# Decay products with gate masks in three bf16 parts in place of one fp32 product

## The reference, cut to what matters

```python
g = -jnp.exp(A_log) * jax.nn.softplus(a + dt_bias)      # one gate per token and value head
def step(S, xs):
    qt, kt, vt, gt, bt = xs
    S = S * jnp.exp(gt)[..., None, None]
    kS = jnp.einsum('bhk,bhkv->bhv', kt, S)
    S = S + bt[..., None, None] * kt[..., :, None] * (vt - kS)[..., None, :]
    o = jnp.einsum('bhk,bhkv->bhv', qt, S)
    return (S, o)
```

## Time and profile before

| | |
|---|---|
| median of 3 runs | 2314.36 us (2313.28 to 2314.37) |
| the profiled execution | 2313.63 us, span 2311.6 us |
| busy: PE | 2015.2 us, 87% |
| busy: DVE | 1538.9 us, 67% |
| busy: ACT | 982.5 us, 43% |
| busy: POOL | 758.4 us, 33% |
| mean granted TensorE clock | 0.962 |

### The profile page before, as it was taken

The page is one execution under the profiler, slowest core; times in us unless marked ns, Lnnn a source line. Parts: engine busy times, 40 slices in busy tenths (PEclk is TensorE's granted clock), DMA queues, the critical chain, the costliest instruction groups (busy, mean ns, idle before and its releaser), DMA issues.

```text
span 2311.6 us, 39665 instructions
## 1 busy us (share of the span) xinstructions
PE 2015.2 (87%) x13026; PEld 1516.7 (66%) x13066; DVE 1538.9 (67%) x2459; ACT 982.5 (43%) x2529; POOL 758.4 (33%) x685
## 2 busy tenths in 40 slices
PE   4578888884588599999999999999999999999996
PEld 2257643334344387878778778787787787877875
DVE  3968841124555577777777777777777777777775
ACT  1012247761010345545445355454454544545544
POOL 4630011102000415336154262361542524615332
PEclk8889989996799799999999999999999999999998
DMA  7446630000011000000000000000000000000001
GB/s 264 147 153 197 196 103 27 18 1 23 23 32 44 25 33 28 14 32 27 9 27 14 32 27 14 23 20 25 27 14 32 27 13 24 18 27 27 14 23 37
DMA packets 72034, 107.37 MB, mean 46 GB/s; under 512 B 22918, under 2 KB 54934, under 8 KB 68790
## 3 DMA queue, kind: packets, MB, share of 16 engines
q1 hardware_dynamic: 64446, 86.60, 12.0%
q10 hardware_dynamic: 4478, 11.88, 1.4%
q0 software_dynamic: 3072, 8.39, 1.1%
HBM read 81.48 MB, written 28.52 MB: 48 GB/s over the span
## 4 chain that ended last, share of the span: by engine, by line
PE 48%; DVE 13%; ACT 3%; issue 3%; POOL 0%; DMA 0%; DVEq 0%; ACTq 0%; POOLq 0%
PE ps L1430 6%; PE ps L1558 5%; PE ps L1550 5%; PE ps L1468 4%; PE ps L1478 3%; DVE P L1961 3%; DVE P_term L1958 3%; DVE conv L1882 3%; PE ps L1615 3%; PE ps L1493 2%; PE ps L1604 2%; PE ps L1564 2%; PE ps L1504 2%; PE ps L1617 2%; PE ps L1591 2%
## 5 line engine op out<-in xcount | busy, mean ns | idle before, releaser
L1882 DVE SCALAR_TENSOR_TENSOR conv<-raw,tap_st,conv 128x1024 f32<-128x1024 f32 x204 | 299.9, 1470 | 3.8
L1430 PE MATMUL ps<-xnT,w_conv_st 128*128 128x512 f32 x544 | 250.4, 599 | 4.4 <-DMA w_conv_st<-in_w_conv 4.4
L1862 POOL TENSOR_TENSOR o<-o,silu_z 128x256 f32<-128x256 f32 x128 | 138.3, 1080 | 255.7 <-DVE silu_z L1902 141.7
L824 DVE TENSOR_REDUCE m_part<-ps 128x1 f32<-128x640 f32 (+7 forms) x176 | 175.1, 1026 | 49.1 <-PE ps L675 32.7
L1756 POOL TENSOR_TENSOR gmask_Q<-upto,g 128x2048 f32<-128x2048 f32 x17 | 61.4, 3610 | 433.7 <-PE ps L1571 433.6
L1635 ACT COPY raw<-ps 128x512 f32<-128x512 f32 x136 | 80.7, 594 | 271.3 <-PE ps L1430 271.3
L990 ACT ACTIVATE probs<-ps 128x1024 f32<-128x1024 f32 (+7 forms) x256 | 146.0, 660 | 44.5 <-PE ps L940 24.1
L1430 PEld LDWEIGHTS ps<-xnT,w_conv_st 128*128 128x128 f32 x544 | 97.7, 191 | 97.2 <-issue 88.6
L1842 POOL TENSOR_TENSOR kq_decayed<-conv,decay_rows 128x1024 f32<-128x1024 f32 x64 | 158.3, 2504 | 0.0
L1478 PE MATMUL ps<-w_z_st,xnT 128*128 128x256 f32 x512 | 148.8, 393 | 0.0
L1468 PE MATMUL ps<-w_out_st,xn_nat 128*128 128x256 f32 x544 | 126.2, 386 | 0.7
(11 more groups left out here) (340 smaller groups left out, 4741.7 us busy)
## 6 DMA issues: line engine op xcount, KB each, us to landing
decay_rows<-scratch_egc SPq DMA_DIRECT2D x17, 1024.0 KB, 4.7
w_conv_st<-in_w_conv SPq DMA_DIRECT2D x17, 512.0 KB, 3.3
scratch_slots_x<-yacc ACTq DMA_DIRECT2D x8, 1024.0 KB, 10.2
slot_rows<-scratch_slots_x SPq DMA_DIRECT2D x16, 512.0 KB, 5.0
scratch_slots_y<-slot_outputs SPq DMA_DIRECT2D x16, 512.0 KB, 3.8
w_gate_up<-in_gu SPq DMA_DIRECT2D x8, 768.0 KB, 8.0
w_gate_up<-in_gu SPq DMA_DIRECT2D x32, 192.0 KB, 3.1
w_out_st<-in_w_out SPq DMA_DIRECT2D x17, 256.0 KB, 2.6
```

The lines of the kernel that those rows point to most:

```text
L824: dve.tensor_reduce(dst, src, AX.X, ALU.max).then_inc(s_max, 1)
L1430: mm = pe.matmul(ps[:, 6 + n % 2, :], wc[:, k, (n // 2) * P:(n // 2 + 1) * P], m.xnT[:, k, (n % 2) * HALF:(n % 2 + 1) * HALF], start=k == ...
L1862: g.tensor_tensor(oc, oc, zs[:, c, :], ALU.mult).then_inc(s_oz, 1)
L1882: op = dve.scalar_tensor_tensor(out=cv[:, t, :], in0=raw[:, t, at:at + T], scalar=tap[:, t, at:at + 1], in1=cv[:, t, :], op0=ALU.mult, op1 ...
```

## The change

The gate is split into three bf16 parts whose sum is the fp32 gate (`g3`: rounded, the rest rounded, the rest of that), once, ahead of the loop, by five VectorE instructions; `after` gets a bf16 copy. `gmask` then makes three masks in place of one, each of 2048 bf16 elements a partition. Two lie in the bytes of `gmask_Q`, the third in those of `xs`. Since `xs` is read longer than `gmask_Q`, GpSimd now waits for the last `QX` products. TensorE sums three bf16 products a bank in place of one fp32 product.

```diff
+        m.g3 = sb("g_parts", [P, 3, NV + 2, NC], BF16)
+        m.afterb = sb("after_bf", [P, P], BF16)
...
+            dve.wait_ge(s_g, 1)
+            step(dve.tensor_copy(m.afterb[:], m.after[:]))
+            step.link(dve.tensor_copy(m.g3[:, 0], m.g[:]))
+            step.link(dve.tensor_tensor(g_rest[:], m.g[:], m.g3[:, 0], ALU.subtract))
+            step.link(dve.tensor_copy(m.g3[:, 1], g_rest[:]))
+            step.link(dve.tensor_tensor(m.g3[:, 2], g_rest[:], m.g3[:, 1], ALU.subtract))
...
+        def gm_part(part):
+
+            if part < 2:
+                return chunks(gm_q[:].rearrange("p e c i -> p (e c) i")).bitcast(BF16)[:, part * 2 * T:(part + 1) * 2 * T]
+            return chunks(xs[:].rearrange("p e c i -> p (e c) i")).bitcast(BF16)
...
-                pe.wait_ge(s_gm, i + 1)
+                pe.wait_ge(s_gm, i * 3 + 3)
...
-                    pe.matmul(ps[:, b, :], m.after[:], chunks(gm_q[:, b // 2, 4 * (b % 2):4 * (b % 2) + 4, :]),
-                              start=True, stop=False)
+                    for part in range(3):
+                        pe.matmul(ps[:, b, :], m.afterb[:], gm_part(part)[:, b * HALF:(b + 1) * HALF], start=part == 0, stop=False)
...
             def gmask(r):
-                gsrc = m.g[:, 0:2, :] if isinstance(r, int) else m.g[:, bass.ds(2 * r, 2), :]
-                g.tensor_tensor(gm_q[:], m.upto[:].unsqueeze(1).unsqueeze(1).broadcast_to([P, 2, NC, P]),
-                                gsrc.unsqueeze(3).broadcast_to([P, 2, NC, P]), ALU.mult).then_inc(s_gm, 1)
+                for part in range(3):
+                    gsrc = m.g3[:, part, 0:2, :] if isinstance(r, int) else m.g3[:, part, bass.ds(2 * r, 2), :]
+                    g.tensor_tensor(gm_part(part).rearrange("p (e c i) -> p e c i", e=2, c=NC),
+                                    m.upto[:].unsqueeze(1).unsqueeze(1).broadcast_to([P, 2, NC, P]),
+                                    gsrc.unsqueeze(3).broadcast_to([P, 2, NC, P]), ALU.mult).then_inc(s_gm, 1)
...
-                pool.wait_ge(s_x, i * ND + ND)
+                pool.wait_ge(s_y, i * ND + ND)
                 gmask(i + 1)
```

More of the change, by code:

```diff
@@ L1062, in stage_l1_inputs @@
         egT = sb("egc_turned", [P, 2, P])
+        g_rest = sb("g_rest", [P, NV + 2, NC])
         in_w = sem("small_in")
```

## The result

The changed kernel takes 2365.3 us (median; 2362.6 to 2370.4) against 2313.8 for the kernel before on the same chip: a ratio of 1.0224, with a 95% interval of 1.0203 to 1.0244. It is slower, as forecast, but by 51 us and not by 18. That lies 6 us under rival 1, "GpSimd wins the tie" (2371).

The account below looks back on a forecast made before the run. TensorE was taken to bound the kernel (87% busy, 48% of the chain). Span 2311.6 + 20.8 - 1.5 - 1.3 = 2329.6 us, plus 2.0 and 0.7, gave 2332 us, 0.8% slower; range 2312 to 2376.

Parts of the forecast that it names:

- rival 1: Before the scan, GpSimd's first mask beats VectorE's second conv instruction: 3.75 us a turn, 60 us, 2371; chance 0.20.
- the tie: Before the scan, GpSimd's first mask comes 0.02 us behind VectorE's second conv instruction; VectorE was taken to win.
- B: VectorE's second conv instruction before the scan, from 2159.96, 1.285 us; forecast to end at 2161.24.
- The chain behind the tie: In scan chunks 0 to 3, the masks delay VectorE's instructions: 1.3 us lost a turn, 16 x 1.3 = 20.8 us.
- the gain of the first step: At the scan's start, the first copy to S goes at 2162.39 and not at 2162.84: 0.45 us gained.
- The masks' duration: On GpSimd, each of the three bf16 masks takes 3.61 us, as the fp32 mask did.
- longer: Rival: GpSimd's masks take 4.0 us, giving 2352, or 4.8 us, giving 2390; chance 0.12 for 4 us and more.
- short, and faster: Rival: GpSimd's masks take 3.0 us and cost the scan nothing: 2305, or 2300; chance 0.13.
- part 1: Head of a turn: bf16 products save TensorE 0.86 us, mostly swallowed; 1.5 us gained in all, 1.3 in the first turn.
- Part 3: Ahead of the loop: five VectorE instructions, 1.8 us, and two more masks, 7.2 us, cost nothing, 0.5 us at most.
- Work given to GpSimd looks free: Whole kernel: GpSimd carries nothing of the chain of waits, so added work there looks free, to be tested in place.

Follow-up runs that it names:

- the kernel with one count more: The changed kernel with one semaphore count on GpSimd's queue between the wait and the first mask: 2322.9 us, ratio 1.0041.
- the kernel with the 0.6 us shift: The changed kernel with its masks also waiting for ScalarE's copy of the last QX products: 2320.7 us, ratio 1.0032.
- the moved masks: Masks made in doubling levels where VectorE uses PSUM: the changed kernel's three bf16 masks, 2310.7 us; the kernel before's one fp32 mask, 2311.1 us.
- The TensorE part alone: The kernel before with three bf16 products a bank, all reading one bf16 mask made at the old place: 2311.1 us, ratio 0.9993.
- the same part added behind the changed queue: The kernel before with GpSimd's queue reordered (2281.1 us), plus three bf16 products a bank of one bf16 mask: 2267.6 us, ratio 0.9803.
- the kernel with the late fp32 mask: The kernel before with its one fp32 mask waiting for the last QX products: 2353.6 us, ratio 1.0175.

## Why the prediction was right and wrong

- **The failed step is the tie.** "I let VectorE win, because L1910 won against L1862 with the same 0.02 us" carried one pair of instructions over to another. L1862 stands 0.02 to 0.03 us behind L1910 in all 16 turns, and VectorE wins each time, in the changed kernel too (L1927 and L1879 there). The mask stands 0.02 us behind B in all 16 turns, just as close as I had worked out, and GpSimd wins each time (the pair reads 6.02). The two ranges of distance overlap, so who wins can't be read off such a distance, and what does decide it stays open. I had both branches and gave this one 0.20. The trace supported no better than even odds, and then the two medians, 2332 and 2371, would have stood side by side.
- **The chain behind the tie was right in kind, and its sizes partly off.** With GpSimd first I had 3.75 us a turn and the trace has 3.38; I had B ending at 1.08 us behind the mask, and it is 1.07. With VectorE first I had 1.3 us a turn, and the kernel with one count more has 0.54. In that branch `S` comes 0.47 and 0.23 us early in chunks 0 and 1, level in chunk 2, and 0.69 and 0.54 late in chunks 3 and 4 (from the kernel with the 0.6 us shift). I had 0.45 and 0.4 early, then 0.3 and 1.3 late.
- **The mis-sized term is the gain of the first step.** In the kernel before, `S` of chunk 1 follows that of chunk 0 by 3.42 us (2162.84 to 2166.26), later ones by 3.65. The scan itself took back 0.23 of the 0.45 us that the mask cost it. I carried all 0.45 along as if it were lost before; the moved masks measure what was really there, 0.21 us a turn.
- **The masks' duration was right**: 3.61 taken, 3.60 measured. So the rivals "longer" and "short, and faster" fall. (The second of these has a slip: with the whole of part 1 reaching the end it comes to 2293 by its own terms, not 2300.) The Trainium skill's 4497 ns for a tensor_tensor of 2048 fp32 elements ("GPSIMD Engine Reference", section 3) does not fit this instruction in either type.
- **Part 1 was right**: 0.86 us a turn saved on TensorE, L1944 "near 1.6" (1.65), L1946 still 2.46, nothing left at its end. The TensorE part alone, and the same part added behind the changed queue, show it from both sides.
- **Part 3**: the five small instructions run in VectorE's wait (of its 3.74 us 1.85 are left), and behind the two more masks of the prologue ScalarE's first `conv` step starts 0.48 us after its last copy of `raw`, as before. Neither has a run of its own. The turns alone give 16 x 3.38 - 1.3 = 52.8 us, and the medians differ by 51.5, so nothing large is left over for them; below a few us that says nothing, since the start of the loop alone differs by up to 7.5 us between the kernels here.
- **"Work given to GpSimd looks free"** was rightly distrusted, but I priced it only at the place where the change had put it. That the same masks might be free 3 to 22 us ahead of the scan could be read from the same trace.

The range of 2312 to 2376 held the time because it reached to the lost tie.

The Trainium skill ("SBUF — State Buffer", Who interferes with whom) states, for VectorE instructions in a two-port mode, that whoever issues first holds the port pair shared by VectorE and GpSimd for its whole instruction, and that the other is blocked. For the forms timed here the runs agree at distances from 0.10 us up. At 0.02 us the records name VectorE as first while GpSimd had the port. A record's start does not settle who came first there.

## What to carry to other kernels

In these runs VectorE instructions with all operands in SBUF and GpSimd's elementwise ones excluded each other for their whole length, so place GpSimd's work in stretches in which VectorE's instructions have a tensor in PSUM, by a wait on the VectorE instruction just before such a stretch: 34 more masks cost 51 us in one place and nothing in another. When two such instructions start within a tenth of a us of each other, give both outcomes near even odds, or better, take the tie away, since one more count in a queue can be worth more than the change. When a gain on the bounding engine doesn't show, look for a fixed appointment behind it (here `kq_decayed`): the same 0.86 us a turn were worth 0 before the queue was reordered and 13.6 us after.

## What the runs showed of the hardware

- **A tie of 0.02 us between VectorE and GpSimd was decided the same way in all 16 turns.** With fp32 and bf16 masks alike taps A and B took 6.01 to 6.03 us where 2.60 is undisturbed, and 0.08 us more turned it round in all 16. At 0.02 to 0.03 us another pair (L1910 and L1862) was decided the other way, in all 16 as well.
- **The clock of TensorE.** After 1.91 us of idle time in a dense stretch the granted clock was 0.50 for 3.4 us in eight of 15 turns of the kernel with the late fp32 mask, and stayed at 1.00 in the other seven, by the same program. In the changed kernel it followed the same idle time in six of 15 scans, and one of 1.8 us at the head of a turn in three. It cost 1.3 to 1.7 us a turn where TensorE was the next thing late, and nothing where VectorE was. What tells the turns with the fall from those without, these runs do not show.
- **GpSimd's elementwise time followed the count of elements and not their type**: 3.60 us for 2048 bf16 results, 3.61 for fp32, 1.90 for 1024.
